# Cross attention in a decoder layer: exponentials moved undivided, results divided instead, and scores in split float32r

## The reference, cut to what matters

```python
q = (query @ Wq.T + bq).reshape(b, lq, HEADS, HEAD_DIM)
k = (key @ Wk.T + bk).reshape(b, lk, HEADS, HEAD_DIM)
v = (value @ Wv.T + bv).reshape(b, lk, HEADS, HEAD_DIM)
scores = jnp.einsum('bqhd,bkhd->bhqk', q * scale, k)
probs = jax.nn.softmax(scores, axis=-1)
attn = jnp.einsum('bhqk,bkhd->bqhd', probs, v).reshape(b, lq, HIDDEN)
return attn @ Wo.T + bo
```

## Time and profile before

| | us |
|---|---|
| median of 3 runs | 2386.76 (2382.62 to 2387.44) |
| the profiled execution | 2381.39 |
| its span, first to last instruction | 2379.6 |
| mean granted clock of TensorE | 0.993 of 2.4 GHz |

### The profile page before, as it was taken

The page is one execution under the profiler, slowest core; times in us unless marked ns, Lnnn a source line. Parts: engine busy times, 40 slices in busy tenths (PEclk is TensorE's granted clock), DMA queues, the critical chain, the costliest instruction groups (busy, mean ns, idle before and its releaser), DMA issues.

```text
span 2379.6 us, 58683 instructions
## 1 busy us (share of the span) xinstructions
PE 2330.8 (98%) x21642; PEld 2033.3 (85%) x21642; DVE 1510.4 (63%) x2563; ACT 1347.2 (57%) x3322; POOL 1399.3 (59%) x1211
## 2 busy tenths in 40 slices
PE   8999989999999999999999999999999899999999
PEld 7888758988888888888888888888888699998998
DVE  4676788836767677676767677676766734435342
ACT  5888852236666666666666666666666642231321
POOL 4777677347667667667666667667665533333332
PEclk9999979999999999999999999999999999999999
DMA  7444478537777777777677777777677831101000
GB/s 190 131 130 120 118 205 321 212 100 195 185 198 199 204 188 203 192 200 208 178 207 193 198 197 197 196 197 204 179 201 198 253 133 36 50 18 66 7 33 24
DMA packets 254825, 384.60 MB, mean 162 GB/s; under 512 B 116760, under 2 KB 132184, under 8 KB 254552
## 3 DMA queue, kind: packets, MB, share of 16 engines
q1 hardware_dynamic: 229976, 330.65, 49.4%
q10 hardware_dynamic: 24576, 50.36, 8.3%
HBM read 126.33 MB, written 40.60 MB: 70 GB/s over the span
## 4 chain that ended last, share of the span: by engine, by line
PE 75%; DVE 1%; issue 1%; ACT 1%; ACTq 0%; POOL 0%; DVEq 0%; POOLq 0%
PE D_ps_p L69 42%; PE D_ps_s L1995 7%; PE D_ps_p L2022 6%; PE E_ps_g L69 6%; PE E_ps_u L69 6%; PE E_ps_d L69 5%; PE E_ps_y L69 3%; ACT D_e L1650 1%; DVE D_columns L1792 0%; PE E_ps_t L2051 0%; ACTq L1666 0%; DVE D_turned L1806 0%; DVE E_stats_a L1849 0%; DVE E_r_a L1865 0%; ACT D_values L1639 0%
## 5 line engine op out<-in xcount | busy, mean ns | idle before, releaser
L1511 POOL TENSOR_SCALAR D_e<-D_e,D_columns 128x722 f32<-128x722 f32 x256 | 538.5, 2103 | 438.1 <-DVE D_columns L1798 437.8
L1792 DVE TENSOR_REDUCE D_columns<-D_ps_s 128x1 f32<-128x723 f32 x512 | 439.7, 899 | 350.2 <-PE D_ps_s L1995 350.0
L1650 ACT ACTIVATE D_e<-D_ps_s,D_columns 128x723 f32<-128x723 f32 x512 | 436.9, 861 | 238.5 <-DVE D_columns L1792 238.5
L1806 DVE STREAM_TRANSPOSE D_turned<-D_e 128x768 f32<-128x768 f32 x512 | 495.5, 972 | 21.1 <-DMA D_pT<-D_turned 20.3
L69 PE MATMUL D_ps_p<-D_ctx_high,cross_wk_high 128*128 128x384 f32 (+1 forms) x1024 | 346.0, 338 | 2.9 <-DVEq L1818 1.5
L69 PE MATMUL D_ps_p<-D_ctx_low,cross_wk_high 128*128 128x384 f32 (+1 forms) x1024 | 333.2, 325 | 0.0
L69 PE MATMUL D_ps_p<-D_ctx_high,cross_wk_low 128*128 128x384 f32 (+1 forms) x1024 | 333.0, 325 | 0.0
L1657 ACT ACTIVATE D_e<-D_e,D_columns 128x722 f32<-128x722 f32 x256 | 230.2, 899 | 59.8 <-DVE D_columns L1798 59.8
L69 PE MATMUL D_ps_p<-cross_wv_high,D_ctx_low 128*128 128x512 f32 (+1 forms) x656 | 257.9, 393 | 0.0
L69 PE MATMUL D_ps_p<-cross_wv_low,D_ctx_high 128*128 128x512 f32 (+1 forms) x656 | 257.7, 393 | 0.0
L69 PE MATMUL D_ps_p<-cross_wv_high,D_ctx_high 128*128 128x512 f32 (+1 forms) x656 | 255.8, 390 | 0.7 <-ACT D_values L1639 0.7
(11 more groups left out here) (264 smaller groups left out, 5225.6 us busy)
## 6 DMA issues: line engine op xcount, KB each, us to landing
D_pT<-D_turned SPq DMA_DIRECT2D x1536, 96.0 KB, 2.7
D_pT<-D_turned ACTq DMA_DIRECT2D x512, 96.0 KB, 2.9
D_craw<-in_ctxT SPq DMA_DIRECT2D x124, 361.0 KB, 4.2
self_v<-wstage SPq DMA_DIRECT2D x25, 256.0 KB, 2.6
A_v<-self_v SPq DMA_DIRECT2D x32, 200.0 KB
self_o<-A_o SPq DMA_DIRECT2D x32, 200.0 KB, 4.1
x<-C_x SPq DMA_DIRECT2D x5, 1280.0 KB, 5.8
cross_q<-C_qo SPq DMA_DIRECT2D x20, 320.0 KB, 4.1
```

The lines of the kernel that those rows point to most:

```text
L1511: pool.tensor_scalar(head, head, inv[:, 2 * (s % 2):2 * (s % 2) + 1], None, ALU.mult)\
L1650: act.activation(e[n // 2 % 2][:, n % 2, 0:PARTS * PART].rearrange("p (a c) -> p a c", a=PARTS), parts_of(n), ACT.Exp, bias=neg_max[:, n % ...
L1792: dve.tensor_reduce(neg_max[:, n % 4:n % 4 + 1], parts_of(n), AX.XY, ALU.max, negate=True)\
L1806: dve.transpose(turned[quad % 2][:, :, 2 * (s % 2) + h, :].rearrange("p j (t r) -> p t j r", r=32), e[s % 2][:, h, :].rearrange("p (t j r) ...
```

## The change

Exponentials are no longer multiplied by the inverse of their sum. They are turned as they are. VectorE turns the four row sums of a quad as well (`turn_sums`) and writes their reciprocals into five columns of each block of `turned` that no query uses (`inverses`), so that they go to `pT` with the same DMAs; `take_result` multiplies the weighted sum by them, and GpSimd adds the values' bias (`add_values_bias`; near the end VectorE does, `take_biased`).

Scores become float32r: queries are split by GpSimd (`block_queries`), keys by ScalarE (high) and VectorE (low, `low_keys`, from the key unit's bank). The parts have 242 keys. A part's four heads run term by term, 36 matmuls per quad.

VectorE's order is now by quad: maxima of the first step, result, maxima of the second, then the turns of the same quad with the low keys between them. ScalarE's order follows. Key units run one quad ahead of their scores rather than three, queries are loaded by quad, moves wait for `scaled` (the multiplied result) rather than for the sum, and context and tail loads change places in SP's list.

```diff
-    PART = -(-S // PARTS)
+    PART = -(-S // (2 * PARTS)) * 2
+    KEYS_AHEAD = 2
+    QUERIES_AHEAD = 3
-    TAIL_STEP = (-2, 1, 2, 3, 6, 6, 9, 9)
+    TAIL_STEP = (-3, 0, 1, 1, 4, 5, 8, 9)
-    PIECE_STEP = (4, 5, 7, 8)
-    FIRST = -6
+    PIECE_STEP = (6, 7, 10, 11)
+    FIRST = -4
...
+        def inverse_of(tile):
+            return tile[:, :, 0, 0:GAP * 32].rearrange("p a (t c) -> p a t c", c=32)[:, :, :, QB:QB + GAP]
...
-                unit_at.setdefault(PAIRS * (b - 1) + u + 2, []).append(("k", b, u))
+                unit_at.setdefault(PAIRS * b + u - KEYS_AHEAD, []).append(("k", b, u))
...
             if kind == "k":
-                pe.wait_ge(k_done, KU * b + n + 1)
+                pe.wait_ge(k_low, KU * b + n + 1)
...
-                pe.wait_ge(o_done, b + 1)
+                pe.wait_ge(scaled, b + 1)
...
                 def move(quad):
                     sp.wait_ge(turn_done, 4 * quad + 4)
-                    wait(sp, pv_done, quad - 1)
+                    sp.wait_ge(inv_done, quad + 1)
+                    wait(sp, scaled, quad - 1)
...
                 for b in range(B - 1):
-                    load_q(b + 1)
                     if b > 0:
                         move(QUADS * b - 1)
+                    load_q(QUADS * b + 3)
+                    if b > 0:
+                        load_ctx(b + 1, 3)
+                    if b % 4 == 1 and b // 4 < FOURS:
+                        load_tails(b // 4, 2)
+                    move(QUADS * b)
+                    load_q(QUADS * b + 4)
                     if b + 2 < B:
                         load_ctx(b + 2, 0)
                         load_ctx(b + 2, 1)
-                    move(QUADS * b)
                     if b % 4 == 1 and b // 4 < FOURS:
-                        load_tails(b // 4, 2)
+                        load_tails(b // 4, 3)
                     if b > 0:
                         store(b - 1)
...
                     move(QUADS * b + 1)
+                    load_q(QUADS * b + 5)
...
-                def normalise_first(s):
-                    pool.wait_ge(inv_done, 2 * s + 1)
...
+                def add_values_bias(quad):
+                    b, m = quad // QUADS, quad % QUADS
+                    pool.wait_ge(scaled, quad + 1)
+                    rows = oo[b % 2][:, m, :]
+                    pool.tensor_scalar(rows, rows, bv_c[:, m:m + 1], None, ALU.add).then_inc(o_done, 1)
...
+                def quad_at(s):
                     if s >= 0:
                         exps(2 * s)
                         exps(2 * s + 1)
+                    take_units("k", s)
+                    if s >= 0:
+                        exps(2 * s + 2)
+                        exps(2 * s + 3)
+                    take_units("k", s + 1)
+                    if s > 1:
+                        move_diagonal(s // 2 - 1)
+                    take_units("v", s)
+                    take_units("v", s + 1)
...
+                def turn_sums(quad):
+                    dve.wait_ge(exp_done, 4 * quad + 4)
+                    wait(dve, inv_done, quad)
+                    dve.transpose(sums, rowsum.unsqueeze(2).broadcast_to([P, BLOCKS, 32])).then_inc(sums_turned, 1)
+
+                def inverses(quad):
+                    dve.wait_ge(sums_turned, quad + 1)
+                    dve.wait_ge(turn_done, 4 * quad + 1)
+                    dve.reciprocal(inverse_of(turned[quad % 2]),
+                                   sums[:, :, 0:QB].rearrange("p j (t c) -> p j t c", c=GAP)).then_inc(inv_done, 1)
...
+                            dve.wait_ge(k_high, KU * b + u + 1)
+                            dve.scalar_tensor_tensor(ks[1][:, m % 2, first:end], bank("k", b, u)[:, 0:end - first],
+                                                     bk_c[:, m:m + 1], ks[0][:, m % 2, first:end].bitcast(F32),
+                                                     ALU.add, ALU.subtract).then_inc(k_low, 1)
...
+                def quad_at(s, first_sum=None):
+                    maxima(s)
                     if s in sum_at:
                         take_result(sum_at[s])
+                    maxima(s + 1)
+                    turn_blocks(s, 0)
+                    low_keys(s)
+                    turn_blocks(s, 1)
+                    turn_blocks(s + 1, 0)
+                    low_keys(s + 1)
+                    turn_sums(s // 2)
+                    if first_sum is not None:
+                        second_sum(0, first_sum)
+                    turn_blocks(s + 1, 1)
+                    inverses(s // 2)
...
+                    def part(a, passed_by=()):
                         first, end = a * PART, min(a * PART + PART, S)
+                        for n, (q, k) in enumerate(SPLIT):
+                            for j in range(4):
+                                rows = slice(HD * j, HD * (j + 1))
+                                last = pe.matmul(of_head[:, j, a, 0:end - first],
+                                                 qs[q][rows, quad % 2, :, :].rearrange("p a q -> p (a q)"),
+                                                 ks[k][rows, quad % 2, first:end],
+                                                 start=(n == 0), stop=(n == len(SPLIT) - 1), tile_position=(HD * j, 0))
```

More of the change, by code:

```diff
@@ L1123, in phase_cross_and_feed_forward @@
         rest = Region(rest_at, nc.sbuf_usable_end)
-        ks = rest("D_keys", [P, QUADS, S])
-        qraw = rest("D_qraw", [P, QUADS, T])
-        qs = rest("D_queries", [P, QUADS, BLOCKS, 32])
+        both_keys = rest("D_keys", [P, 4, S], F32R)
+        ks = [both_keys[:, 2 * part:2 * part + 2, :] for part in range(2)]
+        qraw = rest("D_qraw", [P, 2, T])
+        sums = rest("D_turned_sums", [P, 2 * T])[:, 0:BLOCKS * 32].rearrange("p (j q) -> p j q", j=BLOCKS)
+        qs = Split(rest, "D_queries", [P, 2, BLOCKS, 32])
         vs = [rest("D_values0", [P, ST, D]), None]
@@ L1132, in phase_cross_and_feed_forward @@
         oo = [rest(f"D_o{i}", [P, QUADS, T]) for i in range(2)]
-        columns = rest("D_columns", [P, 5, 4])
-        bk_c, bv_c, neg_max, rowsum, inv = (columns[:, n, :] for n in range(5))
+        columns = rest("D_columns", [P, 4, 4])
+        bk_c, bv_c, neg_max, rowsum = (columns[:, n, :] for n in range(4))
         even = Region(even_at, odd_at)
@@ L1588, in _ @@
                     pool.memset(vs[i][:, ST - 1, :], 0.0).then_inc(consts, 1)
-                pool.memset(qs[:, :, :, :], 0.0).then_inc(consts, 1)
-                pool.wait_ge(consts, 8)
+                for part in range(2):
+                    pool.memset(qs[part][:, :, :, :].bitcast(F32), 0.0).then_inc(consts, 1)
+                pool.wait_ge(consts, 9)
                 pool.wait_ge(all_max, 1)
@@ L1629, in take_keys @@
                     act.wait_ge(u_done, unit_count["k", b, u])
-                    wait(act, s_done, QUADS * (b - 1) + m + 1)
-                    act.activation(ks[:, m, first:end], bank("k", b, u)[:, 0:end - first], ACT.Identity,
-                                   bias=bk_c[:, m:m + 1]).then_inc(k_done, 1)
+                    wait(act, s_done, QUADS * b + m - 1)
+                    act.activation(ks[0][:, m % 2, first:end], bank("k", b, u)[:, 0:end - first], ACT.Identity,
+                                   bias=bk_c[:, m:m + 1]).then_inc(k_high, 1)
                 def take_values(b, i):
@@ L1752, in _ @@
                                 high_of(acts, acts_raw, first_loaded[(n - KD) // 2], n - KD, o_high)
-                step(MAIN)
-                step(MAIN + 1)
+                for s in range(FIRST, MAIN, 2):
+                    quad_at(s)
+                    first_highs(s)
+                    first_highs(s + 1)
+                quad_at(MAIN)
                 def with_weights(tile):
```

216 lines of the change are left out of this document (96 added, 120 removed).

## The result

| | median, us | against the kernel before | profiled execution (span) |
|---|---|---|---|
| before | 2385.45 (2382.62 to 2387.44) | | 2381.39 (2379.6) |
| after | 2442.48 (2436.67 to 2445.93) | 1.0238 (95%: 1.0213 to 1.0262) | 2445.93 (2444.1) |

The changed kernel is 57 us slower; 2430 was forecast, 2364 to 2462 the range.

What follows compares the result with a forecast made beforehand. TensorE, busy 98% of the span, was taken as the bound. Terms -26 + 9 + 46 + 8 + 0 + 6 = +43 us put the profiled execution at 2424, the median at 2430; range 2364 to 2462.

Steps and rivals of the forecast that it cites:

- What bounds the kernel, and who waits: TensorE waits for VectorE's low keys before the first value unit: mostly 0.1 us, 4 to 5 in every fourth batch.
- Scores, -26 us: TensorE's scores, 128 quads: nine float32r sets, 1.22 us from scores to weighted sum instead of 1.44; -26 us (-20 to -35).
- Low keys, +9: VectorE's low keys free the keys' bank later, so each quad's first value unit starts 0.07 late: +9 us (0 to +25).
- D + 5: D is VectorE's first maximum in a quad; the first value unit's load was at D + 4.92, its matmul D + 5.08.
- Turned tiles, +46: SP's late moves delay VectorE's turns, with low keys and value units now behind them: +46 us (+20 to +70).
- six tail loads: Six batches where six tail loads precede the second move: landing D + 17.6, needed D + 12.9, 4.7 late, 28 us.
- the other batches: Seventeen batches where the store, waiting for GpSimd's bias, precedes the second move: 0.35 late on average, 6 us.
- First quads, +8: Phase start: low keys wait behind GpSimd's flag, TensorE idles 4 us, first three quads 1 us each: +8 (+4 to +12).
- The end, 0: Last stretch: four key units (7.8 us) move into it, where TensorE has 9.6 us of room: 0 (-8 to +8).
- The clock, +6: TensorE waits of 4 to 5 us bring half speed some seven times, 1.7 us of work each: +6 (0 to +15).
- VectorE is not the bound: Rival: VectorE's work exceeds 8.9 us per quad by 0.4 or more, short quads wait; 2450 to 2465, chance 0.10.
- The gain that stays: Rival: turns are not late, so the scores' -26 us remains; 2355 to 2381, likeliest 2369, chance 0.22.

Runs made afterwards that it cites:

- e4_low_first: The changed kernel with both low keys before the four turns on VectorE in every fourth quad only: 2396.03 us, ratio 1.0062.
- e6_low_long: The changed kernel with both low keys before the turns on VectorE only in quads with two value units: 2383.94 us, ratio 1.0003.
- e5_queue_f32: e1_queue with only the high x high term of the scores, as plain float32 matmuls: 2402.49 us, ratio 1.0082.
- e2_one_f32: The changed kernel with only the high x high term of the scores, as plain float32 matmuls: 2438.80 us, ratio 1.0247.
- e8_queue_low_ends: e7_queue_low with VectorE's flag after the first low keys and the last activation split behind quad 126's maxima: 2378.40 us, ratio 0.9979.
- e10_start_end: e7_queue_low with both phase ends changed, GpSimd's maximum over partitions later, flag in the fourth quad, quad 126's low keys before turns: 2365.85 us, ratio 0.9931.
- e3_one_f32r: The changed kernel with only the high x high term of the scores, in float32r (three sets of four, not nine): 2405.03 us, ratio 1.0089.
- e1_queue: The changed kernel with the store and tail loads moved behind each batch's second move and its query load in SP's list: 2389.22 us, ratio 1.0023.
- e7_queue_low: The changed kernel with SP's list of e1_queue and VectorE's order of e6_low_long: 2377.69 us, ratio 0.9978.

## Why the prediction was right, point by point

The forecast, 2430, lies 12 us under the 2442.48 measured: +43 was summed up, and the medians moved by 57, the profiled executions by 64.5. The mechanism was the predicted one; the sizes were partly luck, as the term on the turned tiles shows.

**What bounds the kernel, and who waits.** Right: VectorE's low keys in front of the first value unit, with VectorE waiting for the move, in every fourth quad; by e4_low_first and e6_low_long this is not only a reading.

**Scores, -26 us.** The term was right: 1.24 us against 1.22 forecast, sets 0.11 apart. The Trainium skill (TensorE: Matmul & The Clock Gate, LDWEIGHTS) has 107 ns for a load of 128 columns whatever its rows; the trace agrees (0.11 us from set to set). That the saving stays when the move sets the period was not in the sum: where e5_queue_f32 shows 14 us for it, e2_one_f32 shows none. The sum was not hurt by it, because I took the lateness of the turns against the shortened periods. Of e2_one_f32's 19 us that bring the two kernels level, though, only 6 are this mechanism.

**Low keys, +9.** The undisturbed quads are 0.17 shorter where the scores alone give 0.20: 0.03 each, 4 us. The instruction took 0.57 and 0.53 us (0.56 forecast). VectorE's order and the need at D + 5 held; the margin was 0.04 us better.

**Turned tiles, +46.** This is the term that decided, and its place and its order of size were right: 54 us. By class: six tail loads 22 (forecast 28), three tail loads 14 (10), the other batches 18 (6). The last was mis-sized: 0.35 late was forecast and 1.05 came. The working is weaker than its sum. For the six I wrote that a move which starts at D + 6.5 lands at D + 17.6, so in 11.1 us and not in the 10.1 that I said I use; with 10.1 they come to 22, as measured. And 2.95 + 10.1 against 12.9 is 0.15 late, not 0.35; the 0.35 has no row. That 46 lies near 54 is in part two errors that cancel. The room was as forecast (11.0 us from ready to need, 10.9 forecast) and so was the start behind the store (1.16 late in most batches, 0.9 forecast), but the second moves took 8.6 us to issue and 10.5 to land, not the mean of 10.1. Half of that could be read in the trace of before, where the second moves land after 10.26 us and all moves after 10.07. With a margin of tenths I should have used the time of this move, not the mean of all.

**First quads, +8.** The first scores came 18.5 us after the phase's first matmul, before 21.0, although four key units (7.8 us) fewer stand ahead: 5.3 lost, and 0.7 in the first three quads: +6. The flag wait was the first of two late releases; that GpSimd's queries were the next one behind it I had not seen, and e8_queue_low_ends paid for it.

**The end, 0.** From quad 124's scores to the end 553.8 us, before 541.9: 11.9 more, 7.8 of them the moved key units, so +4, within the range given. The output projection now waits 3.25 us for the last low keys: its first matmul starts 0.21 us behind their end, and 0.22 behind it in e10_start_end, where they end sooner.

**The clock, +6.** Right in kind and too small: six falls in the fourth quads, three of them for 6.8 us instead of 3.4, some 13 us.

**Rivals.** VectorE is not the bound of this kernel (969 us busy of the 1210 from 620 to 1830, 80%; 85% was forecast, and e10_start_end, without the waits, has it); e3_one_f32r shows that it is 0.4 us away, as counted. The gain that stays is what e1_queue, e7_queue_low and e10_start_end bring back step by step; 2369 was given for it (its terms add up to 2353 to 2379, not to the 2355 to 2381 written). With the late turn out of TensorE's way, e7_queue_low reaches 2378; what brings it under 2369 are the two ends, which that rival left as they are.

## What to carry to other kernels

When an instruction is put on an engine in front of the critical one, look at what it stands behind in that engine's queue, not only at how long it takes: a wait that had cost nothing for as long as only its own engine stood behind it became the loss of this change (70 us in the fourth quads, 57 in sum), and moving two short operations ahead of it in the long periods took them away. An ordered DMA queue has the same trap one stage earlier: issue what has a deadline first, and what has none, stores and loads for a batch from now, behind it. And a saving on the critical engine can be lost where a late transfer sets the period: the same edit cost nothing with the late turns there and 14 us without them. Mend the wait first, then measure the saving.

## What was not expected of the hardware

GpSimd stands still for 5.7 to 6.2 us in front of its maximum over partitions and again for 6.9 to 7.3 us in front of the first two-operand instruction behind it, in the kernel before too (5.74 and 7.28); casts, and in before copies, which have one operand, run in between without delay (rows of e8_queue_low_ends and e10_start_end above). The Trainium skill (GPSIMD Engine Reference, Instruction dispatch) has about 6 us for the first call of a freshly loaded routine, which fits the first gap. What the engine does in either gap no run here shows.

Half speed does not follow from the length of a wait alone. In after, TensorE's wait of 3.09 us that ended at 865.34 was followed by none, and so was the one of 2.79 us in the rows above; the wait of 2.36 us that ended at 1836.65 was followed by 3.4 us of it, and that of 3.27 us at 772.31 by 6.1. TensorE's timeline and the windows view of two of them:

```profile
865.34 0.50 PE L69 MATMUL D_ps_p<-cross_wv_high,D_ctx_high 128*128 128x512 f32 x1 [3.09 <-DVE D_keys L1857]
...
1836.65 0.79 PE L69 MATMUL D_ps_p<-cross_wv_high,D_ctx_high 128*128 128x512 f32 x1 [2.36 <-DVE D_keys L1857]
```

```profile
862.00:876.00 14.00, 10.91 (x125) 9.18 (x124) 9.07 (x14) 4.23 (x10) 4.35 (x8) 1.00 0.64 169
1833.00:1847.00 14.00, 11.64 (x121) 9.45 (x120) 7.16 (x11) 3.39 (x8) 4.22 (x5) 0.88 0.56 145
```

The same instruction lasts 0.79 us instead of 0.50 where the clock is down.
